# Paired blocks, earlier x loads and a shorter way for the second weights in a two-layer outer-product kernel

## The reference

```python
x0 = xk = x                                   # (b, i, d), B=2048, M=39, D=16
for W in (W0, W1):                            # (39*39, 128) and (39*128, 128)
    Wr = W.reshape(m, Hk, Hn)
    xk = jnp.einsum('bid,bjd,ijh->bhd', x0, xk, Wr)
    outs.append(xk)
return jnp.sum(jnp.concatenate(outs, axis=1), axis=-1)   # (b, 256)
```

## Time and profile before

| | before |
|---|---|
| median of 3 runs | 618.28 us (617.67 to 619.59) |
| profiled execution, its own time | 613.03 us |
| its span, first to last instruction | 610.8 us |
| TensorE busy, mean granted clock | 557.6 us (91%), 0.989 |
| VectorE, ScalarE, GpSimd busy | 76% of the span each |
| DMA moved, mean rate | 150.76 MB, 247 GB/s |

### The profile page before, as it was taken

One profiled execution on the slowest core, in us unless ns is written; L12 is line 12 of the kernel. 1 busy time (PEld: TensorE's weight loads), 2 busy tenths in 40 slices (PEclk: granted clock), 3 DMA queues, 4 the chain that ended last, 5 costly groups with the idle time before them and its releaser, 6 DMA issues.

```text
span 610.8 us, 12886 instructions
## 1 busy us (share of the span) xinstructions
PE 557.6 (91%) x3176; PEld 484.1 (79%) x3176; DVE 466.3 (76%) x806; ACT 465.6 (76%) x980; POOL 462.1 (76%) x404
## 2 busy tenths in 40 slices
PE   1768889999999999999799989999999899999978
PEld 0556767888888888888688878878888788888877
DVE  4858788888888778977678878778978778788630
ACT  4678788888888778877588877778888778888730
POOL 5979899788877787777677877787788678878600
PEclk9979899999999999999999999999999999999999
DMA  8989988877787677777767777687768777878100
GB/s 300 322 315 318 321 291 287 273 258 252 242 279 260 237 260 258 235 253 276 222 228 238 245 261 255 215 281 260 240 240 273 268 240 249 283 256 279 54 30 18
DMA packets 71029, 150.76 MB, mean 247 GB/s; under 512 B 14256, under 2 KB 31024, under 8 KB 70960
## 3 DMA queue, kind: packets, MB, share of 16 engines
q1 hardware_dynamic: 70960, 149.94, 73.0%
HBM read 137.30 MB, written 4.65 MB: 232 GB/s over the span
## 4 chain that ended last, share of the span: by engine, by line
PE 41%; SPq 25%; DMA 11%; issue 8%; POOL 6%; ACT 5%; DVE 4%; ACTq 0%; DVEq 0%; POOLq 0%
SPq L269 16%; DMA xs<-xa_dram 10%; PE acc L359 7%; PE acc L361 6%; PE acc L360 6%; SPq L238 4%; PE fin L399 3%; PE fin L400 3%; PE fin L401 3%; POOL fl L688 3%; PE pg L385 3%; PE pg L386 3%; PE pg L387 3%; POOL fs L683 2%; ACT fh L452 2%
## 5 line engine op out<-in xcount | busy, mean ns | idle before, releaser
L688 POOL TENSOR_TENSOR fl<-fs,fh 128x512 fp32r<-128x512 f32 x192 | 247.5, 1300 | 90.7 <-ACT fh L452 90.6
L359 PE MATMUL acc<-fh,w0h 128*128 128x512 f32 x384 | 164.8, 429 | 39.5 <-ACT x L473 25.8
L584 DVE TENSOR_TENSOR fp<-xl,xr 128x512 f32<-128x512 f32 x192 | 133.5, 696 | 63.5 <-ACT xl L459 54.1
L683 POOL TENSOR_TENSOR fs<-xr,xs 128x512 f32<-128x512 f32 x128 | 163.0, 1292 | 8.2 <-DMA xr<-xb_dram 6.8
L361 PE MATMUL acc<-fl,w0h 128*128 128x512 f32 x384 | 153.6, 400 | 0.0
L360 PE MATMUL acc<-fh,w0l 128*128 128x512 f32 x384 | 152.7, 398 | 0.0
L588 DVE TENSOR_TENSOR fl<-fp,fh 128x512 fp32r<-128x512 f32 x192 | 131.4, 685 | 22.9 <-ACT fh L452 21.0
L602 DVE TENSOR_TENSOR gl<-pg,gh 128x320 fp32r<-128x320 f32 x256 | 118.9, 486 | 30.8 <-ACT gh L492 27.5
L452 ACT ACTIVATE fh<-fp 128x512 fp32r<-128x512 f32 x192 | 114.3, 595 | 33.3 <-PE acc L361 31.2
L452 ACT ACTIVATE fh<-fs 128x512 fp32r<-128x512 f32 x192 | 121.5, 633 | 18.8 <-PE acc L361 15.1
L492 ACT ACTIVATE gh<-pg 128x320 fp32r<-128x320 f32 x256 | 106.3, 434 | 22.2 <-PE pg L387 21.5
(11 more groups left out here) (38 smaller groups left out, 684.6 us busy)
## 6 DMA issues: line engine op xcount, KB each, us to landing
xr<-xb_dram SPq DMA_DIRECT2D x192, 512.0 KB, 5.7
xs<-xa_dram SPq DMA_DIRECT2D x64, 256.0 KB, 4.7
xbd<-xdhl SPq DMA_DIRECT2D x512, 20.0 KB, 3.6
xp<-xpairs_dram SPq DMA_DIRECT2D x32, 256.0 KB, 2.8
xdr<-xd_dram SPq DMA_DIRECT2D x64, 80.0 KB, 2.5
w_copy<-w_dram SPq DMA_DIRECT2D x6, 384.0 KB, 5.6
w1l<-w_copy SPq DMA_DIRECT2D x6, 384.0 KB, 4.4
out_dram<-outs SPq DMA_DIRECT2D x8, 256.0 KB, 5.8
```

The costliest lines, as they stand in the source:

```text
L359: nc.tensor.matmul(acc[:, :], w0h[:, t, :], fh[:, t, :], start=t == 0, stop=False)
L584: nc.vector.tensor_tensor(f_at(t), xl[:, :], xr[:, gi % 2, t, :], ALU.mult).then_inc(prod_dve, 1)
L683: nc.gpsimd.tensor_tensor(f_at(t), xr[:, gi % 2, t, :], xs[:, gi % 2, :], ALU.mult)\
L688: nc.gpsimd.tensor_tensor(fl[:, t, :], f_at(t), fh[:, t, :], ALU.subtract).then_inc(low_pool, 1)
```

## The change

- **Blocks.** `xd` holds each value twice as wide, with a zero beside it, so one DMA writes a square of two b (32 rows, 2560 bytes each) with its zeros: 4 DMAs of 80 KB in place of 8 of 20 KB. The load of `xdr` grows from 80 to 160 KB, its two halves are now the two b, so it is a single buffer; the splits are 128x320 and no longer 128x160. The load of group g+2 waits until group g+1 has been split, and stands at the end of SP's slot.
- **x first.** SP issues `load_x` ahead of the right rows, once the products 0 and 4 of the group before are made, and no longer behind r1.
- **GpSimd.** The products 1 and 4 of group g+1 come ahead of `low(g, 5)`.
- **Prologue.** r1 of group 0 is loaded ahead of the second part of W0; group 0's highs, lows and products are ordered anew around it.
- **Second weights.** No copy from HBM to HBM. 10 pieces of 4 rows (256 KB) come through `outs`, the output buffer, one at a time: `w1_load(p)` waits for the low part of piece p-1. `final` waits for the pieces that it needs, not for all.

```diff
-NW = 6
+NW = 4
...
+def pieces_before(row):
+    return min(-(-row // NW), PIECES)
...
-        xdhl = sb("xdhl", [P, 2, NQ, 2, MI], F32R)
+        xdhl = sb("xdhl", [P, 2, 2, NQ, 2, MI], F32R)
...
+        def w1_raw(p):
+            rows = outs[:, :, :].rearrange("p a b -> p (a b)").rearrange("p (n h) -> p n h", h=H)
+            return rows[:, 0:piece(p).stop - piece(p).start, :]
...
-            def load_xd(g, gi):
-                sp.dma_start(xdr[:, gi % 2, :, :], xd[g]).then_inc(xd_in[gi % 2], 16)
+            def load_xd(g):
+                sp.dma_start(xdr[:, :, :, :], xd[g]).then_inc(xd_in, 16)
 
             def w0_load(k):
                 ts = slice(W0_PART * k, W0_PART * k + W0_PART)
                 sp.dma_start(w0a_raw[k], w0a[:, ts, :]).then_inc(w0a_in[k], 16)
                 sp.dma_start(w0b_raw[k], w0b[:, ts, :]).then_inc(w0b_in[k], 16)
 
-            def w1_move(p):
-                sp.dma_start(w1_copy[:, piece(p), :], w1[:, piece(p), :]).then_inc(w1_moved, 16)
-
             def w1_load(p):
-                sp.wait_ge(w1_moved, 16 * (p + 1))
                 if p:
-                    sp.wait_ge(w1_in, 16 * p)
-                sp.dma_start(w1l[:, piece(p), :].bitcast(F32), w1_copy[:, piece(p), :]).then_inc(w1_in, 16)
+                    sp.wait_ge(w1_ready, p)
+                sp.dma_start(w1_raw(p), w1[:, piece(p), :]).then_inc(w1_in, 16)
 
             def blocks(g, gi, first):
                 if first and gi < 2:
@@ -264,10 +267,10 @@
                 else:
                     sp.wait_ge(g_done, NQ * (g - 1))
                 s = gi % 2
-                for b in range(BQ):
-                    rows = slice(D * b, D * b + D)
-                    sp.dma_start(xbd[rows, s, b, :, :, :].rearrange("p q s i -> p (q s i)").bitcast(F32),
-                                 xdhl[rows, s, :, :, :].rearrange("p q s i -> p (q s i)").bitcast(F32))\
+                for b in range(0, BQ, 2):
+                    rows = slice(D * b, D * b + 2 * D)
+                    sp.dma_start(xbd[rows, s, b:b + 2, :, :, :].rearrange("p b q s i -> p (b q s i)").bitcast(F32),
+                                 xdhl[rows, s, :, :, :, :].rearrange("p b q s i -> p (b q s i)").bitcast(F32))\
                       .then_inc(xbd_in[s], 16)
...
                     more3 = not (last and gi + 3 >= CB)
-                    sp.wait_ge(xd_low, g + 1)
                     if more3:
                         wait_product(sp, g + 1, 0)
-                        wait_product(sp, g + 1, 1)
+                        wait_product(sp, g + 1, 4)
+                        load_x(j, gi + 3)
                         load_right(j, gi + 3, 0)
                     blocks(g, gi, first)
-                    if more2:
-                        load_xd(g + 2, gi)
                     if gi % 2 == 0 and more2:
                         sp.wait_ge(sq_ready, CP * j + gi // 2 + 1)
                         load_pair(CP * j + gi // 2 + 1)
                     if more3:
                         wait_product(sp, g + 1, 3)
                         load_right(j, gi + 3, 1)
-                    if first and gi < PIECES:
-                        w1_load(gi)
-                        if gi + 1 < PIECES:
-                            w1_move(gi + 1)
                     if more3:
-                        wait_product(sp, g + 1, 4)
-                        load_x(j, gi + 3)
                         wait_product(sp, g + 1, 5)
                         load_right(j, gi + 3, 2)
+                    if not (last and gi + 1 >= CB):
+                        sp.wait_ge(xd_low, g + 2)
+                    if more2:
+                        load_xd(g + 2)
+                    if first or second and g + 1 < PIECES:
+                        w1_load(g + 1)
                     if gi == 2 and not (first or second):
                         send(j - 2)
 
             w0_load(0)
             load_x(0, 0)
             load_right(0, 0, 0)
+            load_right(0, 0, 1)
             w0_load(1)
-            load_right(0, 0, 1)
             load_right(0, 0, 2)
             load_pair(0)
-            load_xd(0, 0)
-            load_xd(1, 1)
+            load_xd(0)
             load_x(0, 1)
             load_right(0, 1, 0)
             sp.dma_start(idn[:, :], ident).then_inc(ident_in, 16)
@@ -322,15 +322,17 @@
             sp.wait_ge(w0_ready, 3)
             load_right(0, 1, 2)
             wait_product(sp, 0, 0)
-            wait_product(sp, 0, 1)
+            wait_product(sp, 0, 4)
+            load_x(0, 2)
             load_right(0, 2, 0)
             wait_product(sp, 0, 3)
             load_right(0, 2, 1)
-            wait_product(sp, 0, 4)
-            load_x(0, 2)
             wait_product(sp, 0, 5)
             load_right(0, 2, 2)
-            w1_move(0)
+            sp.wait_ge(xd_low, 1)
+            load_xd(1)
+            sp.wait_ge(w0_sum, 1)
+            w1_load(0)
...
-                    if fresh:
-                        pe.wait_ge(w1_ready, PIECES)
-                    else:
+                    if not fresh:
                         pe.wait_ge(out2_ready, c)
+                if fresh:
+                    pe.wait_ge(w1_ready, pieces_before(rows[-1] + IB))
...
                     if more:
                         xd_split(j, gi + 1, first and gi == 0)
+                    if (first or second) and 0 < g <= PIECES:
+                        w1_high_part(g - 1)
+                    if more:
                         high(g + 1, 4, False)
                         high(g + 1, 3, False)
-                    if first and 0 < gi <= PIECES:
-                        w1_high_part(gi - 1)
                     if more:
...
             act.wait_ge(w0_sum, 1)
             nc.scalar.activation(w0h[:, 0:W0_PART, :], w0a_raw[0], COPY).then_inc(w0_high, 1)
             left_out(0, 0, True)
+            high(0, 0, True)
+            high(0, 1, True)
+            high(0, 2, True)
             act.wait_ge(w0_sum, 2)
             nc.scalar.activation(w0h[:, W0_PART:NT, :], w0a_raw[1][:, 0:NT - W0_PART, :], COPY).then_inc(w0_high, 1)
-            high(0, 0, True)
             nc.scalar.activation(x1th[:, 0:2, :], w0a_raw[1][:, NT - W0_PART:W0_PART, :], COPY).then_inc(w0_high, 1)
             nc.scalar.activation(w0q[:, :, :], w0b_raw[1][:, NT - W0_PART:W0_PART, :], COPY).then_inc(w0_high, 1)
-            high(0, 1, True)
-            high(0, 2, True)
-            xd_split(0, 0, True)
             high(0, 4, True)
             high(0, 3, True)
+            xd_split(0, 0, True)
             high(0, 5, True)
             left_out(0, 1, False)
...
+            product(0, 0, 0, True)
+            low(0, 0)
+            product(0, 0, 2, True)
+            product(0, 0, 3, True)
+            low(0, 2)
             dve.wait_ge(w0a_in[1], 16)
             dve.wait_ge(w0b_in[1], 16)
             two = w0a_raw[1][:, 0:NT - W0_PART, :]
             nc.vector.tensor_tensor(two, two, w0b_raw[1][:, 0:NT - W0_PART, :], ALU.add).then_inc(w0_sum, 1)
-            product(0, 0, 0, True)
+            product(0, 0, 5, True)
             dve.wait_ge(w0_high, 2)
             nc.vector.tensor_tensor(w0l[:, W0_PART:NT, :], two, w0h[:, W0_PART:NT, :], ALU.subtract)\
               .then_inc(w0_ready, 1)
-            product(0, 0, 2, True)
-            low(0, 0)
-            product(0, 0, 3, True)
+            low(0, 3)
             dve.wait_ge(w0_high, 4)
             last_lo = w0b_raw[1][:, NT - W0_PART:W0_PART, :]
             nc.vector.tensor_tensor(last_lo, last_lo, w0q[:, :, :], ALU.subtract).then_inc(w0_sum, 1)
-            product(0, 0, 5, True)
             dve.wait_ge(w0_sum, 3)
             nc.vector.tensor_tensor(w0q[:, :, :], last_lo, x1th[:, 0:2, :], ALU.add).then_inc(w0_ready, 1)
-            low(0, 2)
-            low(0, 3)
...
                     g = CB * j + gi
                     more = not (last and gi == CB - 1)
-                    low(g, 5)
                     if more:
                         product(j, gi + 1, 1, False)
                         product(j, gi + 1, 4, False)
+                    low(g, 5)
+                    if more:
                         low(g + 1, 1)
                         xd_split(g + 1, gi + 1)
+                    if (first or second) and 0 < g <= PIECES:
+                        w1_low_part(g - 1)
+                    if more:
                         low(g + 1, 4)
                     if gi == 5 and not first:
                         first_out(j - 1, not odd)
-                    if first and 0 < gi <= PIECES:
-                        w1_low_part(gi - 1)
...
             product(0, 0, 1, True)
+            low(0, 1)
             product(0, 0, 4, True)
-            low(0, 1)
             xd_split(0, 0)
             low(0, 4)
...
+
+    xd = np.zeros((NG, P // (2 * D), 2, D, 2, NQ, MI), x.dtype)
+    for v in range(2):
+        xd[:, :, v, :, v] = xo.reshape(NG, NQ, P // (2 * D), 2, D, MI)[:, :, :, v].transpose(0, 2, 3, 1, 4)
+    xd = xd.reshape(NG, P, 2, NQ, MI)
```

(48 more changed lines are left out.)

## The result

The changed kernel takes 658.14 us (median of 4 runs, 657.75 to 659.25), the kernel before 618.93 us beside it (617.67 to 620.03). The ratio is 1.0637, 95% interval 1.0611 to 1.0664. That is 39 us slower, where I forecast 23 us slower and a range up to 655: the sign and the place were right, the size was not.

A forecast was written before the change was run, and what follows sets the result against it. SP's queue, 8.98 us a slot against TensorE's 8.63, was taken to bound the full slots by delaying xs. Late start 31.4 + 4.2 less 12.5 regained is 23.1 us, on 618.28 gives 641.4 us; 80% range 617 to 655.

The forecast's parts named there:

- T0: End of SP's slot 0, after the new prologue: the xdr load of group 2 is issued there, at 28.0 us.
- landing L behind r1 and r2: Time from issue to landing of the xdr load, queued behind 1 MB: 4.9 us, ends 2.1 and 6.8.
- splits, low part, hand-overs: After xdr lands: ScalarE's split 0.45 us, GpSimd's 0.88, the weights' low part 1.3, hand-overs 0.12; together 2.75.
- SP's part: SP's issues after its wait for weights: w1, x, r0, blocks, xp every second slot, r1, r2; 5.3 us with waits.
- period of the ring: Weight pieces 1 to 9, one a slot: xdr landing, splits, low part, then SP's issues run in series, 12.95 us.
- xd(10) issued to FULL(10): End of the weight loading: landing, splits, low parts, two GpSimd products and four matmuls take 13.75 us.
- FULL(10) to FULL(11): One more period, less 0.3 us for the short last piece: 12.65 us against 8.44, so 4.2 us later.
- gained from FULL(11) to FULL(63): Full slots: with four fewer block issues and x first, xs waits go, returning 12.5 of 13.0 us.
- 10 C - 106.4: Whole change in us, C being the period of the ring: each microsecond of the xdr load's landing counts ten times.
- the later stalls and their cause: Full slots: TensorE loses 13.0 us because xs is late, SP's slot of 8.98 us exceeding TensorE's 8.63.
- the rival by which SP's issues weren't the limit: Full slots: the ring holds and nothing comes back later, 12.5 us more, 654 us in all; chance 7%.
- GpSimd's order at nothing: Full slots: low(g, 5) comes two products, 2.6 us, later but isn't needed until main's last tile; no effect.

The follow-up runs named there:

- Run 3: Changed kernel, with the xdr load behind the blocks and ahead of xp, r1 and r2 in slots 1 to 9, wait for weights unmoved: 637.05 us, ratio 1.0322.
- run 2: Changed kernel, with the xdr load first in SP's slot in slots 1 to 9, wait for weights unmoved: 637.38 us, ratio 1.0319.
- run 1: Changed kernel, with SP loading piece g of the second weights at the end of slot g, not piece g+1: 609.17 us, ratio 0.9853.
- run 4: Changed kernel, with ScalarE's wait for xdr and split moved behind x1_out of the next slot while the weights come in: 662.65 us, ratio 1.0715.
- run 7: Kernel before, only with x loaded ahead of r0, both behind the products 0 and 4: 616.27 us, ratio 0.9971.
- run 9: Kernel of run 1 without the two reorderings (GpSimd's low(g,5) first, x behind r1 again): 606.91 us, ratio 0.9813.
- Run 6: Kernel of run 1, with each pair of blocks sent as two DMAs, eight block issues a slot at unchanged bytes: 678.1 us, ratio 1.0992.
- run 8: Kernel before, only with GpSimd's products 1 and 4 ahead of low(g,5): 617.82 us, ratio 0.9999.
- run 5: Kernel of run 1, with the prologue of the kernel before on all engines: 607.38 us, ratio 0.9836.
- run 10: Kernels of run 1 and Run 3 together: piece g at the end of slot g, xdr load ahead of xp, r1 and r2: 606.08 us, ratio 0.9822.

## Why the prediction was right in kind and too small

| step | predicted | measured in after's trace |
|---|---|---|
| T0, xdr load of group 2 | 28.0 us | 28.18 |
| landing L behind r1 and r2 | 4.9 | 6.2 to 7.3, median 6.6 |
| splits, low part, hand-overs | 2.75 | 2.67 (49.59 to 52.26) |
| SP's part | 5.3 | 5.0 (37.99 to 42.95), 5.9 with xp |
| period of the ring | 12.95 | 14.69 (28.18 to 145.71, eight) |
| xd(10) issued to FULL(10) | 13.75 | 19.93 |
| its landing alone | 4.9 | 7.4 |
| FULL(10) to FULL(11) | 12.65 | 13.42 |
| gained from FULL(11) to FULL(63) | 12.5 | 12.8 |
| tail | 0 | 2.4 lost |

FULL(11) comes 179.06 - 122.41 = 56.65 us late, where I had 35.6. Two steps make the difference, the first of them most of it.

**"The block has just this place in the queue, with a little more ahead of it: I take L = 4.9" was mis-sized.** The xdr load lands after 6.6 us, near the 6.8 of r2 itself in the earlier trace rows and not the 5.0 of the 20 KB block behind it. Both rows were there; I took the one with the same place, but the load is eight times the block. The other terms of the ring came out as forecast (8.0 us, where I had 8.05), so the period is 1.74 us longer, eight times: 13.9 us. The load of xd(10) itself landed after 7.4 us, which is 2.5 us more. Run 3 bears out that the landing counts once a slot: it was 5.1 us there, and the period was the sum round the ring with it. In run 2 it was 2.9 us, and the period fell until another ring held.

**"Then GpSimd reaches `low(10,4)`, two products, `low(10,5)`" failed as a step.** I followed GpSimd's queue to FULL(10). The trace shows another path. The end of the last period, after, and the busy time of the stretch that follows:

```profile
153.17 0.47 ACT L482 ACTIVATE xdhl<-xdr 128x320 fp32r<-128x320 f32 x1 [4.91 <-DMA xdr<-xd_dram]
...
156.10 0.58 ACT L475 ACTIVATE x<-acc 128x512 f32<-128x512 f32 x1
...
156.74 0.50 PE L361 MATMUL acc<-fh,w0h 128*128 128x512 f32 x1 [4.16 <-ACT x L475]
...
159.47 1.28 POOL L691 TENSOR_TENSOR fl<-fs,fh 128x512 fp32r<-128x512 f32 x1
```

```profile
156.74:160.40 3.66, 3.66 (x12) 3.18 (x13) 3.38 (x7) 2.78 (x6) 3.66 (x4) 0.59 0.91 280
```

ScalarE waits in order: `x1_out(9)` stands behind the split of xd(10), the weights' high part, three highs and `left_out`. So TensorE can't begin slot 10 before 156.74, and the slot itself takes 8.9 us, to FULL(10) at 165.64. The same work, first `main` matmul to FULL, took 7.32 us in slot 12 (180.17 to 187.49), where TensorE didn't stop and the granted clock was 1.00. So some 1.6 us of the 8.9 are the clock: it was 0.59, mostly at its lower level (1.2 GHz), in the first 3.66 us behind the stop of 4.16 us. GpSimd was on time: `low(10,5)` ended at 160.75, 7.6 us behind the landing where I had 7.95, and with the four matmuls FULL(10) would have been at some 161.7. The path over ScalarE and TensorE is 4.0 us longer, 1.6 of them the clock, once, since it isn't in the ring. I had asked only what is queued behind the wait on SP. From the load of xd(10) to FULL(10) it is 6.2 us more than my 13.75: 2.5 of landing, and 3.7 of path. 13.9 + 6.2 + 0.1 (T0 and rounding) = 20.2 us, and 0.8 more in the slot to FULL(11): the 21 us missing, of which some 16 are the landing (13.9 + 2.5). The landing's part rests on runs 1 and 3; the path's 3.7 us were read from the trace, and no run shows them, since run 4 moved that delay and didn't take it out.

With the measured 6.7 us (mean) for L my own formula, 10 C - 106.4, gives 41 us and 659. That this meets the median of 658.14 is partly luck: between the traces the change was 46.3 us, with the longer path and the tail in it.

**Right:** the ring and its members (run 1 opens it and gives 49 us); the later stalls and their cause, SP's issue count (run 7: another order gives nothing; run 9: fewer issues alone give 12.0 us), so the rival by which SP's issues weren't the limit falls. Run 6 shows what eight issues cost beside a single xdr buffer, and isn't a repeat of the stalls of before, which were for xs. The Trainium skill (DMA: Bandwidth & Descriptors, "Issuing engines are not separate DMA queues") calls the sequencer's time for a DMA "usually small relative to the DMA itself"; for a single block that is so here, 0.62 us to issue and 5.0 us to land. What I drew from it, a gain of about 0, is not: the 13 or 14 issues of a slot added up to 8.98 us, the longest queue, and 12.8 us came back with four fewer. Right as well: the xdr split at 0.876 us (0.88 predicted); GpSimd's order at nothing (run 8); slots of 8.43 us from FULL(11) on, in the loops 8.63. The prologue's T0 was right, but run 5 shows that its delay costs little in itself.

**The tail's 2.4 us** I didn't foresee. It goes with the granted clock, 0.88 against 1.00 in the same work: in both traces TensorE has the same three stops there, 1.41, 0.61 and 1.05 us, and only in after's was the clock lower behind the first of them (0.64 from 633.4 to 640.0; before, 1.00 throughout). The tails of runs 1, 2 and 3 were 26.7 to 26.8 us, those of 4 and 10 28.1 to 28.2, and that of run 8, the kernel before but for GpSimd's order, 28.95 at 0.88. So it isn't peculiar to this change, and the 2.4 us can't be put down to it. Why the clock fell there stays open.

## What to carry to other kernels

A wait's price can be more than the time to its releaser: it is the length of the ring that it closes. Before moving a wait, write down for each in-order queue what was issued just ahead of it and whether the releaser needs that. If it does, the period is the sum round the ring, and asking for the same thing one slot later took 81.6 us of waits down to 1.9 here (run 1). Take a load's landing from rows of its size as well as of its place: 160 KB behind 1 MB landed like the 512 KB ahead of it (6.6 and 6.8 us) and not like a 20 KB block (5.0). And follow every in-order engine that waits, ScalarE here, to the instruction that the bottleneck needs. Where one queue was the limit, reordering it moved the wait to another load (run 7), and fewer issues paid (run 9).

## What the runs showed of the hardware

- An issue's cost on SP didn't go by bytes. From SBUF to SBUF the 80 KB blocks of after (L272) took 0.59 us in the median, as the 20 KB ones of before (L269); from HBM the loads of 160, 256 and 512 KB in after took 0.33 to 0.42 us each in the median.
- The 160 KB load of xdr landed in 2.9 us first in SP's slot (run 2), in 5.1 us behind the blocks (run 3) and in 6.6 us behind r1 and r2 (after), all medians.
- In after, the granted clock was 0.59 in the 3.66 us behind a stop of 4.16 us. It made 8.90 us of a slot's work that took 7.32 at 1.00 in slot 12. The ring didn't get longer by it, since TensorE isn't in it.
- The added bytes aren't free on the DMA engines. Full slots went from a share of 0.77 at 258 GB/s to 0.90 at 289, and in run 1's start 0.94 go with 300 GB/s, where before 0.98 went with 354. Over the whole span run 1's 163 MB took 83.6% of 606.5 us, before's 150 MB 73.0% of 610.8: 61 us of all 16 engines for 13 MB more. I had put 287 under 354 and called it nothing; in full slots it was nothing, and whether it holds the start is open (run 10).
